# Last layer of a two-layer kernel: the down products of the experts with the weights stationary and 512 rows moving, and the row groups as the outer loop of an expert

## The chip, the cores and the metric

One NeuronCore of a Trainium2 chip runs the whole program. The metric is device time in microseconds of one execution, as the median of several runs. Names of engines: PE is TensorE, DVE is VectorE, ACT is ScalarE, POOL is GpSimd, SP is SyncE, whose queue issues most transfers.

## The reference

The program computes two layers over x of 8 x 256 rows (2048 rows, 16 tiles of 128) and 256 columns. The first layer is an attention with gates and a routed mixture of 32 experts. The second is a long convolution with two small networks, and after it a dense mixture of 8 experts, in which each row goes through every expert. The change touches that last part alone:

```python
x = hidden_states
router_probs = softmax(x @ w_router)
gate_weights = softmax(x @ w_gating / GATE_TEMP)
g = einsum('bsh,ehf->ebsf', x, w_gate)
u = einsum('bsh,ehf->ebsf', x, w_up)
h = silu(g) * u
expert_out = einsum('ebsf,efh->ebsh', h, w_down)
cw = router_probs * gate_weights
cw = cw / (sum(cw, axis=-1, keepdims=True) + 1e-09)
out = einsum('ebsh,bse->bsh', expert_out, cw)
```

The hidden width is F = 1024 per expert. The input of this part is a layer norm of x, and the result is added to x.

## The kernel before

The program is written engine by engine, with the order of every engine's instructions set by hand and semaphores between them. The last layer is reached after some 700 us.

Each expert's three matrices lie in DRAM cut into four chunks of 256 hidden units (128 x 1536 numbers: gate, up, down). A chunk is loaded by SP into one of two slots of `wS` (`load`, L423), rounded to a high half `wH` by ACT (`split_high`, L1371), and POOL takes the rest as a low half `wL` (`split_low`, L1680). Every matrix product is made of three passes (high by high, high by low, low by high) with operands of type fp32r.

The loop of the last layer counts chunks, in pairs. For each chunk come the four groups of 512 rows, and for each group the chunk's two halves of 128 hidden units. One such half for one group is a step: 32 chunks x 8 = 256 steps. A step has

- on PE an up part (`up`, L1969): twelve products, weights stationary (128 x 128), 512 rows of the transposed input `xTH`/`xTL` moving, six for the gate into a bank of PSUM and six for the up matrix into another;
- on ACT a silu of the gate (`silu`, L1376) into `sg`;
- on DVE (`expert_step`, L1226, and `expert_low`, L1236) the product `hF`, its rounded half `hH` and the rest `hL`;
- on PE a down part (`down`, L1987): for each of the four row tiles of the group three products with `hH` or `hL` stationary and 256 columns of the down matrix moving, so that the sums come out with rows on partitions.

The two halves of a chunk are summed in PSUM. DVE then takes each tile's sums, times that row's router weight (a number per partition, `cw2`), and adds them to x (`mixed`, L1242), two tiles in each step. PE's order puts the ups of step s+2 ahead of the downs of step s (`experts`, L2264), so ACT and DVE have a step and more of time.

```python
for q, (h, w, s) in enumerate(((hH, wH, sH), (hL, wH, sH), (hH, wL, sL))):
    last = pe.matmul(o, h[:, b, t * P:(t + 1) * P], piece(w, s, slot, col, D),
                     start=(opens and t % 2 == 0 and q == 0), stop=(closes and q == 2), skip_group_check=True)
```

A wait of the ups asks that the product `hF` of two steps before is done, since its PSUM bank is written again. A wait of the downs asks for that step's low half. Ahead of the first steps PE still turns the last group's normalised rows (`turn("L", 3)`, L2278) and makes the router's logits of tiles 8 to 15 in two batches (`router_logits`, L2276 and L2283). After the last step DVE adds the last four tiles, and SP stores x in four pieces as the groups get ready.

## Time and profile before

| what | value |
|---|---|
| median of three runs | 1789.19 us (1787.07 to 1790.77) |
| the profiled execution | 1789.22 us |
| its span, first to last instruction | 1787.1 us |
| mean granted clock of PE | 0.967 |
| busy: PE, DVE, ACT, POOL | 93%, 67%, 27%, 25% |
| matmuls, weight loads | 9760, 9761 |

The span is what the trace shows; 2 us lie around it. Views of the trace that are used here: the page (busy times, clock), tables by stretches of time (busy time of each engine and the granted clock), the timeline (one row per instruction or run of equal instructions: start, length, engine, line, output<-inputs, shape), and the list of transfers. A matmul's length in the timeline contains time that overlaps with the next one, so PE's pace is read from start to start. The weight loads of PE have rows of their own (PEld) beside the matmuls.

### The profile page before, as it was taken

What the parts mean: (1) busy time and instruction counts of PE and PEld (TensorE: products, weight loads), DVE (VectorE), ACT (ScalarE), POOL (GpSimd) and SP (SyncE); (2) the same over time, 40 slices, a digit from 0 to 9 for tenths busy, and PEclk for the clock granted to TensorE, in tenths of its full rate; (3) what the DMA queues carried; (4) which work ended last, traced back from release to release, by engine and by line L of the source; (5) the groups of instructions that cost most, each with busy time, mean ns of one, the idle gap of its engine ahead of it and who ended that gap; (6) DMA issues with size and microseconds to landing.
All of it is one profiled execution on the core that took longest, in us unless ns stands there. A gap on an engine that the chain in (4) does not pass through costs nothing.

```text
span 1787.1 us, 29075 instructions
## 1 busy us (share of the span) xinstructions
PE 1662.3 (93%) x9760; PEld 1424.1 (80%) x9761; DVE 1203.4 (67%) x2477; ACT 478.7 (27%) x844; POOL 449.1 (25%) x297
## 2 busy tenths in 40 slices
PE   6999987698957798999999999999999999999998
PEld 5896663388845687888888888888888888888887
DVE  6666787466656795666666766766766766766765
ACT  4455332143422464211211211211111111111111
POOL 2551257688436601100100100100100100100100
PEclk9998998799978997999999999999999999999999
DMA  6993031388643200010000000000000000000001
GB/s 199 276 340 145 24 113 50 106 248 262 204 132 106 69 1 19 19 36 18 19 34 18 20 32 18 20 33 18 21 31 18 23 30 18 26 26 18 18 0 48
DMA packets 72003, 127.51 MB, mean 71 GB/s; under 512 B 8320, under 2 KB 51776, under 8 KB 71808
## 3 DMA queue, kind: packets, MB, share of 16 engines
q1 hardware_dynamic: 38096, 84.31, 14.6%
q10 hardware_dynamic: 27696, 25.51, 4.5%
q0 software_dynamic: 6144, 16.79, 2.9%
q8 instruction: 43, 0.70, 0.2%
q14 instruction: 24, 0.20, 0.0%
HBM read 82.54 MB, written 44.04 MB: 71 GB/s over the span
## 4 chain that ended last, share of the span: by engine, by line
PE 78%; POOL 6%; issue 5%; DMA 5%; DVE 4%; ACT 1%; SPq 0%; POOLq 0%; DVEq 0%; another core or an unknown queue 0%; ACTq 0%
PE ps L1982 39%; PE ps L1998 20%; PE ps L2089 4%; DMA slots_in<-xn,idS 3%; PE ps L2108 2%; POOL slots_in L1710 2%; POOL yg L1749 2%; PE ps L1781 2%; PE ps L2069 1%; PE ps L2186 1%; DMA yg<-slots_out,idG 1%; DMA x<-in_x 1%; PE ps L1851 1%; PE ps L1850 1%; PE ps L2164 1%
## 5 line engine op out<-in xcount | busy, mean ns | idle before, releaser
L1982 PE MATMUL ps<-xTH,wH 128*128 128x512 f32 x1024 | 402.8, 393 | 1.5 <-DVE hF L1231 1.5
L1982 PE MATMUL ps<-xTH,wL 128*128 128x512 f32 x1024 | 402.2, 393 | 0.0
L1982 PE MATMUL ps<-xTL,wH 128*128 128x512 f32 x1024 | 399.1, 390 | 0.0
L1379 ACT ACTIVATE sg<-ps 128x512 f32<-128x512 f32 x264 | 157.9, 599 | 884.2 <-PE ps L1982 884.2
L1231 DVE TENSOR_TENSOR hF<-sg,ps 128x512 f32<-128x512 f32 x256 | 175.9, 687 | 303.8 <-ACT sg L1379 303.8
L1682 POOL TENSOR_TENSOR wL<-wS,wH 128x1536 fp32r<-128x1536 f32 x32 | 111.8, 3495 | 961.1 <-ACT wH L1374 961.1
L1998 PE MATMUL ps<-wL,hH 128*128 128x256 f32 x1024 | 289.8, 283 | 0.0
L1998 PE MATMUL ps<-wH,hL 128*128 128x256 f32 x1024 | 289.7, 283 | 0.0
L1998 PE MATMUL ps<-wH,hH 128*128 128x256 f32 x1024 | 288.6, 282 | 0.5 <-DVE hL L1240 0.5
L1240 DVE TENSOR_TENSOR hL<-hF,hH 128x512 fp32r<-128x512 f32 x256 | 258.4, 1009 | 0.1
L1982 PEld LDWEIGHTS ps<-xTL,wH 128*128 128x128 f32 x1024 | 192.8, 188 | 42.2
L1250 DVE SCALAR_TENSOR_TENSOR x<-ps,cw,x 128x256 f32<-128x256 f32 x512 | 222.7, 477 | 1.0 <-PE ps L1998 1.0
L1982 PEld LDWEIGHTS ps<-xTH,wH 128*128 128x128 f32 x1024 | 193.8, 189 | 35.7 <-ACT sg L1379 1.4
L1982 PEld LDWEIGHTS ps<-xTH,wL 128*128 128x128 f32 x1024 | 193.9, 189 | 30.6
L1998 PEld LDWEIGHTS ps<-wH,hH 128*128 128x128 f32 x1024 | 195.5, 191 | 10.6 <-DVE hL L1240 0.7
L1998 PEld LDWEIGHTS ps<-wH,hL 128*128 128x128 f32 x1024 | 195.5, 191 | 9.9
L1998 PEld LDWEIGHTS ps<-wL,hH 128*128 128x128 f32 x1024 | 195.5, 191 | 0.0
L1234 DVE CAST hH<-hF 128x512 fp32r<-128x512 f32 x256 | 109.4, 427 | 36.7 <-PE ps L1998 28.0
L1710 POOL DMA_INDIRECT slots_in<-xn,idS x64 | 74.6, 1166 | 60.5 <-DMA slots_in<-xn,idS 30.7
L1781 PE MATMUL ps<-maskT,idb 128*128 128x384 bf16 x348 | 73.6, 343 | 15.6 <-DVE x L973 15.6
L2089 PE MATMUL ps<-eHL,hH 128*128 x384 | 81.5, 295 | 2.4 <-POOL eHL L1697 2.4
L1749 POOL DMA_INDIRECT yg<-slots_out,idG x48 | 51.2, 1067 | 71.1 <-DMA slots_out<-yo 49.0
(396 smaller groups left out, 2440.1 us busy)
## 6 DMA issues: line engine op xcount, KB each, us to landing
wS<-in_w SPq DMA_DIRECT2D x32, 768.0 KB, 4.2
slots_in<-eS SPq DMA_DIRECT2D x16, 768.0 KB, 10.6
eS<-in_wr SPq DMA_DIRECT2D x32, 384.0 KB, 4.1
xl<-slots_in ACTq DMA_DIRECT2D x48, 256.0 KB, 3.8
slots_out<-yo ACTq DMA_DIRECT2D x48, 256.0 KB, 3.0
k_parts<-parts SPq DMA_DIRECT2D x8, 512.0 KB, 5.6
q_parts<-parts SPq DMA_DIRECT2D x8, 512.0 KB, 3.9
stackA<-k_parts SPq DMA_DIRECT2D x24, 128.0 KB, 5.6
```

Source lines behind the costliest of these rows:

```text
L1231: dve.tensor_tensor(hF[:, b, :], sg[:, b, :], ps[:, 2 + b, :], ALU.mult).then_inc(mul_done, 1)
L1234: dve.tensor_copy(hH[:, b, :], hF[:, b, :]).then_inc(h_high, 1)
L1240: dve.tensor_tensor(hL[:, b, :], hF[:, b, :], f32(hH[:, b, :]), ALU.subtract).then_inc(h_low, 1)
L1250: dve.scalar_tensor_tensor(x[:, tile, :], acc, cw2[:, tile, bass.ds(it, 1)], x[:, tile, :], ALU.mult, ALU.add).then_inc(evac_done, 1)
L1379: act.activation(sg[:, b, :], ps[:, b, :], ACT.Silu).then_inc(silu_done, 1)
L1682: pool.tensor_tensor(blocks(wL, slot, plain), blocks(wS, slot, plain), f32(blocks(wH, slot, plain)), ALU.subtract).then_inc(w_low, 1)
L1710: pool.indirect_dma_start(xs_d, bass.IndirectOffsetOnAxis(ap=idS[:, n, k:k + 1], axis=0), xn[:, n, :], None, bounds_check=TILES * P - 1, o ...
L1749: pool.indirect_dma_start(slot_rows(n)[:, k, :], None, ys_d, bass.IndirectOffsetOnAxis(ap=idG[:, n, k:k + 1], axis=0), bounds_check=TILES ...
L1781: pe.matmul(ps[:, bank, 0:384], idb[:, :], maskT[:, :], start=True, stop=True)
L1982: last = pe.matmul(ps[:, 2 * half + b, :], piece(w, s, slot, col, P), v[:, k, g * 512:(g + 1) * 512], start=q == 0, stop=q == 5)
L1998: last = pe.matmul(o, h[:, b, t * P:(t + 1) * P], piece(w, s, slot, col, D), start=(opens and t % 2 == 0 and q == 0), stop=(closes and q = ...
L2089: last = pe.matmul(ps[:, 2 + b, t * D:(t + 1) * D], h[:, b, (2 * t + k) * P:(2 * t + k + 1) * P], eFlat[:, bass.ds(off + (w + k * D), D)], ...
```

## The change

The down part is turned round: the down matrix's 128 x 128 blocks are the stationary operand, and 512 rows of `hH` or `hL` move, six products a step. The sums come out transposed, with columns on partitions, and eight halves (all 1024 hidden units of an expert) are summed in PSUM for one group before they are read. For this the loops of an expert change places: the four groups are the outer loop and the eight halves the inner one, and all four chunks of the expert stay on the chip, in `wH`/`wL` and two new buffers `wH2`/`wL2` that take the place of older tensors.

DVE multiplies the sums by the router's weights, now along the free dimension (`cwB`, the expert's 2048 weights on every partition), and adds them to transposed sums `yT` in SBUF (`weigh`, `add`), in three steps of every eight. `cwB` comes from DRAM: the weights `cwc` are turned once on PE, copied by ACT, stored, and SP loads one line of 8 KB to all partitions for each expert. In the last expert PE turns the sums back (`turn_out`, eight transposes for each group) and DVE adds them to x (`add_out`); its last group keeps the old form of the down products. The first steps change their order too: the turning of the last rows and the logits, now one batch for tiles 8 to 15, stand later.

```diff
+        def chunk_high(c):
+
+            return wH[:, 1 - c, :] if c < 2 else wH2[:, c - 2, :]
...
+            def load_weights_of(e):
+
+                rows = cw_d.rearrange("(e n) p -> e (n p)", n=NT)
+                src = rows[e:e + 1] if isinstance(e, int) else rows[bass.ds(e, 1)]
+                sp.dma_start(cwB[:, :], src.to_broadcast([P, NT * P])).then_inc(cw_moved, 16)
+
+            load_chunks(0)
+            sp.wait_ge(turned_copied, 5)
+            sp.dma_start(cw_d, cwT[:, :]).then_inc(cw_moved, 16)
+            sp.wait_ge(cw_moved, 16)
+            load_weights_of(0)
+            with sp.Fori(1, E1) as e:
+                load_chunks(e)
+                sp.wait_ge(mix_read, e * 8)
+                load_weights_of(e)
...
+            def weigh(e, g, dt):
+
+                if dt == 0:
+                    dve.wait_ge(down_done, e * 32 + (8 * U_L1 + 8 * g + 8))
+                    dve.wait_ge(cw_moved, e * 16 + 32)
+                dve.tensor_tensor(tm[:, dt, :], ps[:, 4 + 2 * (g % 2) + dt, :], cwB[:, g * 512:(g + 1) * 512], ALU.mult).then_inc(mix_read, 1)
+
+            def add(e, g, dt, first):
+
+                dve.wait_ge(mix_read, e * 8 + (2 * g + dt + 1))
+                if first:
+                    dve.tensor_copy(yT[:, g, dt, :], tm[:, dt, :]).then_inc(sum_added, 1)
+                else:
+                    dve.wait_ge(sum_added, e * 8 + (2 * g + dt - 7))
+                    dve.tensor_tensor(yT[:, g, dt, :], yT[:, g, dt, :], tm[:, dt, :], ALU.add).then_inc(sum_added, 1)
...
+            def add_out(k, half):
+
+                g = (k + 3) % 4
+                dve.wait_ge(out_turned, k + 1)
                 for t in (2 * half, 2 * half + 1):
-                    tile = pair % 4 * 4 + t
-                    acc = ps[:, 4 + 2 * (pair % 2) + t // 2, (t % 2) * D:(t % 2) * D + D]
-                    dve.scalar_tensor_tensor(x[:, tile, :], acc, cw2[:, tile, bass.ds(it, 1)], x[:, tile, :],
-                                             ALU.mult, ALU.add).then_inc(evac_done, 1)
+                    acc = ps[:, 4 + 2 * (g % 2) + t // 2, (t % 2) * D:(t % 2) * D + D]
+                    dve.tensor_tensor(x[:, 4 * g + t, :], acc, x[:, 4 * g + t, :], ALU.add).then_inc(out_ready, 1)
...
+            def replace(e, c):
+
+                act.wait_ge(down_done, e * 32 + (8 * U_L1 - 32 + 24 + 2 * c + 2))
+                chunk_split(e, c)
+
+            def expert(e, first=False, last=False):
+                for s in range(32):
+                    silu(e * 32 + (8 * U_L1 + s), s % 2, PLAIN)
+                    if not first and s in (0, 2):
+                        replace(e, 2 + s // 2)
...
+                    if not last and s in (28, 30):
+                        replace(e + 1, (s - 28) // 2)
...
+                else:
+                    for dt, w, h, q in ((0, high, hH, 0), (0, low, hH, 1), (1, high, hH, 0), (1, low, hH, 1), (0, high, hL, 2), (1, high, hL, 2)):
+                        done = pe.matmul(ps[:, pair + dt, :], w[:, col + dt * P:col + (dt + 1) * P], h[:, b, :], start=(ft == 0 and q == 0),
+                                         stop=(ft == 7 and q == 2), skip_group_check=True)
+                done.then_inc(down_done, 1)
+
+            def turn_out(k):
+
+                g = (k + 3) % 4
+                pe.wait_ge(sum_added, 8 * (E1 - 1) + 2 * k)
+                for dt in range(2):
+                    for t in range(4):
+                        done = pe.transpose(ps[:, 4 + 2 * (g % 2) + t // 2, (t % 2) * D + dt * P:(t % 2) * D + (dt + 1) * P],
+                                            yT[:, g, dt, t * P:(t + 1) * P], ident[:, :])
+                done.then_inc(out_turned, 1)
+
+            def expert(e, first=False, last=False):
+
+                for s in range(32):
+                    if s < 30:
+                        expert_up(e, s + 2)
                     elif not last:
-                        expert_up(it + 1, local - 14)
-                    expert_down(it, local)
+                        expert_up(e + 1, s - 30)
+                    if first and s == 0:
+                        pe.wait_ge(logits_read, 1)
+                    if first and s == 8:
+                        pe.wait_ge(turned_copied, 5)
+                    expert_down(e, s, last)
+                    if first and s == 1:
+                        pe.wait_ge(evac_done, 4 * M_L1)
+                        turn("L", 3, bank=6)
+                    if first and s == 2:
+                        router_logits(6, 8, 8)
+                    if first and s == 5:
+                        pe.wait_ge(cw_done, 2)
+                        pe.transpose(ps[:, 7, 0:P], cwc[:, :, :].rearrange("p e n -> p (e n)"), ident[:, :]).then_inc(turned_done, 1)
+                    if last and s % 8 == 3:
+                        turn_out(s // 8)
```

PE, a step in the middle of the last layer, before: the last ups and the first three down products, which are there four times (L1982 is `up`, L1998 is `down`).

```order
L1982 MATMUL ps<-xTH,wL 128x512
L1982 MATMUL ps<-xTL,wH 128x512
L1998 MATMUL ps<-wH,hH 128x256
L1998 MATMUL ps<-wH,hL 128x256
L1998 MATMUL ps<-wL,hH 128x256
```

The same place now, with all the down products of the step (L2369 is `expert_up`, L2392 is the new form in `expert_down`) and the first up of the next:

```order
L2369 MATMUL ps<-xTH,wL 128x512
L2369 MATMUL ps<-xTL,wH 128x512
L2392 MATMUL ps<-hH,wH 128x512 [waits h_low]
L2392 MATMUL ps<-hH,wL 128x512
L2392 MATMUL ps<-hH,wH 128x512
L2392 MATMUL ps<-hH,wL 128x512
L2392 MATMUL ps<-hL,wH 128x512 x2
L2369 MATMUL ps<-xTH,wH_198 128x512 [waits mul_done,silu_done]
```

The ups stand as they stood; twelve products of 256 columns have become six of 512, and the one wait of the downs stays that for the low half.

DVE, one step in the loop before: the product, its rounded half, the two additions to x (L1250) and the low half, with the waits.

```order
L1231 TENSOR_TENSOR hF<-sg,ps 128x512 [waits silu_done]
L1232 REGISTER_ALU
L1234 CAST hH<-hF 128x512 [waits down_done,mul_done]
L1250 ISA [waits evac_done,down_done]
L1250 SCALAR_TENSOR_TENSOR x<-ps,cw_71,x 128x256
L1250 ISA
L1250 SCALAR_TENSOR_TENSOR x<-ps,cw_71,x 128x256
L1240 TENSOR_TENSOR hL<-hF,hH 128x512 [waits h_high]
```

DVE now, steps 9 to 11 of an expert, in which the first group's sums are taken (L1289 is `weigh`, L1298 is `add`):

```order
L1276 CAST hH<-hF 128x512 [waits down_done,mul_done]
L1289 TENSOR_TENSOR tm<-ps,cwB 128x512 [waits cw_moved,down_done]
L1282 TENSOR_TENSOR hL<-hF,hH 128x512 [waits h_high]
L1273 TENSOR_TENSOR hF<-sg,ps 128x512 [waits silu_done,h_low]
L1276 CAST hH<-hF 128x512 [waits down_done,mul_done]
L1289 TENSOR_TENSOR tm<-ps,cwB 128x512
L1298 TENSOR_TENSOR yT<-yT,tm 128x512 [waits sum_added,mix_read]
L1282 TENSOR_TENSOR hL<-hF,hH 128x512 [waits h_high]
L1273 TENSOR_TENSOR hF<-sg,ps 128x512 [waits silu_done,h_low]
L1276 CAST hH<-hF 128x512 [waits down_done,mul_done]
L1298 TENSOR_TENSOR yT<-yT,tm 128x512 [waits sum_added,mix_read]
L1282 TENSOR_TENSOR hL<-hF,hH 128x512 [waits h_high]
```

The two additions of every step are gone; four instructions in three of eight steps stand in their place, and the first of them waits for the load of the router's weights, ahead of that step's low half.

ACT at the end of an expert in the loop: before, one chunk was split in every eight steps; now the exchange of the chunks begins behind the silu of steps 28 and 30 (L1615 is `chunk_split`), and two more follow in the next expert.

```order
L1690 ISA
L1614 REGISTER_ALU [waits down_done]
L1615 ACTIVATE wH<-wS 128x1536 [waits stage1_loaded]
L396 REGISTER_ALU
L1455 REGISTER_ALU [waits mul_done]
L1456 ACTIVATE sg<-ps 128x512 [waits up_done]
L396 REGISTER_ALU
L1455 REGISTER_ALU [waits mul_done]
L1456 ACTIVATE sg<-ps 128x512 [waits up_done]
L1690 REGISTER_ALU
L1614 REGISTER_ALU [waits down_done]
L1615 ACTIVATE wH<-wS 128x1536 [waits stage0_loaded]
```

Two splits, two steps apart, and each waits for a down product of the expert that ends, since it overwrites that expert's chunk.

## Rows read from the trace of the kernel before

**Rows 1.** Page, part 1: engine, busy us (share of the span), instructions.
```profile
PE 1662.3 (93%) x9760; PEld 1424.1 (80%) x9761; DVE 1203.4 (67%) x2477; ACT 478.7 (27%) x844; POOL 449.1 (25%) x297
```
**Rows 2.** Table by stretches: us, each engine's busy us, clock, DMA share, GB/s.
```profile
1000.00:1200.00 200.00, 200.00 (x1149) 176.44 (x1149) 136.26 (x240) 36.55 (x54) 20.98 (x6) 1.00 0.07 24
```
**Rows 3.** Timeline of PE, one step: start, length, engine, line, operation.
```profile
1000.77 0.40 PE L1982 MATMUL ps<-xTH,wH 128*128 128x512 f32 x1
...
1003.52 0.28 PE L1998 MATMUL ps<-wH,hH 128*128 128x256 f32 x1
1003.63 0.28 PE L1998 MATMUL ps<-wH,hL 128*128 128x256 f32 x1
...
1004.95 0.40 PE L1982 MATMUL ps<-xTH,wH 128*128 128x512 f32 x1
```
**Rows 4.** Timeline of PE, 24 ups in a row, then 16 logit products.
```profile
701.49 0.40 PE L1982 MATMUL ps<-xTH,wH 128*128 128x512 f32 x1
...
704.26 0.39 PE L1982 MATMUL ps<-xTH,wH 128*128 128x512 f32 x1
...
706.98 0.18 PE L2209 MATMUL ps<-wg1HL,xTH 128*128 128x32 f32 x1
...
708.57 0.26 PE L2210 MATMUL ps<-wg1HL,xTL 128*128 128x16 f32 x1
```
**Rows 5.** Timeline of ACT and DVE beside that step.
```profile
999.54 0.60 ACT L1379 ACTIVATE sg<-ps 128x512 f32<-128x512 f32 x1 [3.58 <-PE ps L1982]
1000.17 0.69 DVE L1231 TENSOR_TENSOR hF<-sg,ps 128x512 f32<-128x512 f32 x1 [1.50 <-ACT sg L1379]
1001.04 0.43 DVE L1234 CAST hH<-hF 128x512 fp32r<-128x512 f32 x1 [0.18 <-PE ps L1998]
1001.38 0.87 DVE L1250 SCALAR_TENSOR_TENSOR x<-ps,cw,x 128x256 f32<-128x256 f32 x2
1002.17 0.68 DVE L1240 TENSOR_TENSOR hL<-hF,hH 128x512 fp32r<-128x512 f32 x1
```
**Rows 6.** Timeline of ACT and POOL, the two halves of one chunk.
```profile
1020.93 1.48 ACT L1374 ACTIVATE wH<-wS 128x1536 fp32r<-128x1536 f32 x1
1022.49 3.50 POOL L1682 TENSOR_TENSOR wL<-wS,wH 128x1536 fp32r<-128x1536 f32 x1 [29.94 <-ACT wH L1374]
```
**Rows 7.** List of transfers: count, KB each, median us from issue to landing.
```profile
wS<-in_w SPq DMA_DIRECT2D x32, 768.0 KB, 4.2
...
x<-in_x SPq DMA_DIRECT2D x2, 1024.0 KB, 14.3
FW<-in_fw SPq DMA_DIRECT2D x1, 1024.0 KB, 6.8
```
**Rows 8.** First expert: timeline of PE, and the table's row of that stretch.
```profile
710.00:715.00 5.00, 3.94 (x12) 2.96 (x11) 3.68 (x10) 2.44 (x5) 0.00 (x0) 0.50 0.01 3
711.95 0.77 PE L1982 MATMUL ps<-xTH,wH 128*128 128x512 f32 x1 [1.06 <-DVE hF L1231]
...
716.82 0.28 PE L1998 MATMUL ps<-wH,hH 128*128 128x256 f32 x1
...
729.07 0.40 PE L1982 MATMUL ps<-xTH,wH 128*128 128x512 f32 x1
```
**Rows 9.** Timeline of PE, eight transposes and the two matmuls behind them.
```profile
694.59 1.03 PE L2146 MATMUL ps<-ident,xnL 128*128 128x128 f32 x8
695.38 0.48 PE L2164 MATMUL ps<-xTH,fH 128*128 128x512 f32 x1
695.69 0.39 PE L2164 MATMUL ps<-xTH,fL 128*128 128x512 f32 x1
```
**Rows 10.** Timeline of PE and DVE, the last downs and additions.
```profile
1779.57 0.28 PE L1998 MATMUL ps<-wL,hH 128*128 128x256 f32 x1
1780.38 0.39 PE L1998 MATMUL ps<-wH,hH 128*128 128x256 f32 x1 [0.54 <-DVE hL L1240]
...
1782.12 1.66 DVE L1250 SCALAR_TENSOR_TENSOR x<-ps,cw,x 128x256 f32<-128x256 f32 x4 [1.00 <-PE ps L1998]
```

More of the change, by code:

```diff
@@ L1272, in _ @@
-            for part in range(13, 16):
-                mixed(N_L1 // 2 - 1, part // 2, part % 2)
+            body(1)
+            with dve.Fori(2, E1 - 1) as e:
+                body(e)
+            body(E1 - 1, last=True)
+            dve.wait_ge(down_done, 8 * U_L1 + 32 * E1)
+            dve.wait_ge(out_ready, 16)
+            for t in range(4):
+                tile = 12 + t
+                acc = ps[:, 6 + t // 2, (t % 2) * D:(t % 2) * D + D]
+                dve.scalar_tensor_tensor(x[:, tile, :], acc, cwc[:, E1 - 1, tile:tile + 1], x[:, tile, :], ALU.mult, ALU.add).then_inc(out_ready, 1)
@@ L1761, in _, with chunk_rest @@
                 add_residual(g)
-            split_low(U_L1, 1)
+            def chunk_rest(e, c):
+                pool.wait_ge(w_high, e * 4 + (U_L1 + c + 1))
+                pool.tensor_tensor(chunk_low(c), wS[:, 1 - c % 2, :], f32(chunk_high(c)), ALU.subtract).then_inc(w_low, 1)
+            chunk_rest(0, 0)
             add_residual(3)
-            def experts(it, last):
-                split_low(it * 2 + (U_L1 + 1), 0)
-                if not last:
-                    split_low(it * 2 + (U_L1 + 2), 1)
-            with pool.Fori(0, N_L1 // 2 - 1) as it:
-                experts(it, False)
-            experts(N_L1 // 2 - 1, True)
+            pool.wait_ge(residual_added, 4)
+            pool.wait_ge(normed["B"], 16)
+            for c in range(1, 4):
+                chunk_rest(0, c)
+            with pool.Fori(1, E1) as e:
+                for c in range(4):
+                    chunk_rest(e, c)
         @block.tensor
@@ L2255, in _, with expert_up @@
             block("B", 3, {3: ("L", 2)}, 0)
-            def expert_up(it, local):
-                up(it * 16 + (8 * U_L1 + local), local, it * 2 + (U_L1 + local // 8), 1 - local // 8, PLAIN)
-            def expert_down(it, local):
-                down(it * 16 + (8 * U_L1 + local), local, it * 8 + (M_L1 + local // 2), 1 - local // 8, local // 2 % 2,
-                     local % 2 == 0, local % 2 == 1)
-            def experts(it, last):
-                for local in range(16):
-                    if local < 14:
-                        expert_up(it, local + 2)
-                    elif not last:
-                        expert_up(it + 1, local - 14)
-                    expert_down(it, local)
+            def expert_up(e, s):
+                n, g, ft, b = e * 32 + (8 * U_L1 + s), s // 8, s % 8, s % 2
+                if g == 0 and ft % 2 == 0:
+                    pe.wait_ge(w_low, e * 4 + (U_L1 + ft // 2 + 1))
+                pe.wait_ge(silu_done, n - 1)
+                wait(pe, mul_done, n - 1 - PLAIN)
+                high, low = chunk_high(ft // 2), chunk_low(ft // 2)
+                for half in range(2):
+                    q = 0
+                    for k in range(2):
+                        col = half * BLK + k * D + ft % 2 * P
+                        for w, v in ((high, xTH), (low, xTH), (high, xTL)):
+                            last = pe.matmul(ps[:, 2 * half + b, :], w[:, col:col + P], v[:, k, g * 512:(g + 1) * 512], start=q == 0, stop=q == 5)
+                            q += 1
+                last.then_inc(up_done, 1)
@@ new lines, in expert_down @@
+            def expert_down(e, s, last=False):
+                n, g, ft, b = e * 32 + (8 * U_L1 + s), s // 8, s % 8, s % 2
+                pair = 4 + 2 * (g % 2)
+                wait_low(pe, n + 1)
+                if ft == 0:
+                    wait(pe, mix_read, e * 8 + (2 * g - 2))
+                    if last:
+                        wait(pe, out_ready, 4 * g)
+                high, low = chunk_high(ft // 2), chunk_low(ft // 2)
+                col = 2 * BLK + ft % 2 * D
+                if last and g == 3:
+                    for t in range(4):
+                        o = ps[:, pair + t // 2, (t % 2) * D:(t % 2 + 1) * D]
+                        for q, (h, w) in enumerate(((hH, high), (hL, high), (hH, low))):
+                            done = pe.matmul(o, h[:, b, t * P:(t + 1) * P], w[:, col:col + D], start=(ft == 0 and t % 2 == 0 and q == 0),
+                                             stop=(ft == 7 and q == 2), skip_group_check=True)
+                else:
+                    for dt, w, h, q in ((0, high, hH, 0), (0, low, hH, 1), (1, high, hH, 0), (1, low, hH, 1), (0, high, hL, 2), (1, high, hL, 2)):
+                        done = pe.matmul(ps[:, pair + dt, :], w[:, col + dt * P:col + (dt + 1) * P], h[:, b, :], start=(ft == 0 and q == 0),
+                                         stop=(ft == 7 and q == 2), skip_group_check=True)
+                done.then_inc(down_done, 1)
```

152 lines of the change are left out of this document (81 added, 71 removed).

## Prediction

> **What bounds the kernel now.** I read the views from the coarse to the fine. The page's list of engines has TensorE (PE) busy for 93% of the span [rows 1]. The table by stretches then shows the stage that the change rewrites: PE is busy in every microsecond at a granted clock of 1.00, the upper of its two levels (2.4 GHz), while VectorE (DVE) works 68% of the time and ScalarE (ACT) and GpSimd (POOL) under 20% [rows 2]. What is worth anything here is therefore PE's own pace, and the timeline gives it. A step (one chunk's 128 hidden units of 512 rows) starts at 1000.77, its down part at 1003.52, the next step at 1004.95 [rows 3]: 2.75 us for twelve up products of 512 columns, 1.43 us for twelve down products of 256, 4.18 us together. 256 such steps, some 1070 us, are 60% of the span. Start to start, the ups take 229 ns on the mean and the downs 119; the matmul's own "us" column overlaps its neighbours and is not used for sums.
>
> **Two prices hide in these 229 and 119 ns.** The first down product after a run of ups takes 0.11 us, not 0.12 [rows 3]. And where 24 ups follow each other with nothing between, the first twelve, which come straight after 256-column products, take 2.77 us (701.49 to 704.26), and the second twelve 2.72 (to 706.98) [rows 4]: 231 ns, then 227. So I read 227 ns as what 512 columns cost, and half of it, 113, as what 256 cost. A run of 256-column products is paced by something else, at 120 ns, and leaves a debt that the next ups pay with a few ns each. Both the 7 ns and the debt belong to the short products.
>
> **The downs, steady part.** The change turns twelve products of 256 columns into six of 512, for all steps but the last group's eight. By 227 ns a step costs 18 x 0.2267 (2.72 / 12) = 4.080 us against 4.180, 0.100 less. The three first steps are counted below, the eight last keep the old form, so 245 steps give **-24.5 us**. Bounds: if the ups kept their 229 ns and the downs took the same, 18 x 0.229 = 4.122 and the gain is 14.2 us; if all eighteen ran at the 231 ns of the first half of [rows 4], it is 5.4 us.
>
> One rule speaks against so much. By the Trainium skill ("TensorE: Matmul & The Clock Gate", Back-to-back issue gap) a matmul at the full clock costs its columns over 2.4 GHz and a fixed 2.5 ns, so halving the number of products would save only six times 2.5 ns a step, an estimated 3.7 us in all. The trace does not agree in the fixed part: 256 columns cost 120 ns in the run and 512 cost 227, a difference of 13 ns for a pair.
>
> **DVE, off the path.** It loses two additions from PSUM a step (0.87 us) and gets, per eight steps, two weighted copies of 128x512 out of PSUM and two sums in SBUF. Nearest rows: the product that reads PSUM, 0.69, and the subtraction in SBUF, 0.68 [rows 5]. That is 2.7 us per eight steps against 7.0. Its worst step then has 0.69 + 0.43 + 0.68 + 1.4 = 3.2 us of work in 4.08. The low half is ready at 1002.85 and its down starts at 1003.52 + 4.18 = 1007.70, 4.85 us later; a later half by 0.5 us is covered. Nothing.
>
> **Weights, off the path.** Before, a chunk served 33 us; now all four are exchanged around the border of two experts. In PE's steps: chunk 0 is released after step 25, ACT splits it after the silu of step 28, POOL makes its low half, and its first up stands at the start of what would be step 30. The silu of step 28 ends about 3.5 us into step 26 (it begins 0.2 us after its ups and takes 0.60 [rows 5]); with 1.48 and 3.50 us [rows 6] the low half is there 0.5 us into step 28, 6.2 us early. Chunks 1 to 3 follow two steps apart with the same margin. The load of chunk 2 may start when the low half of chunk 0 is done and must land before ACT wants it, some 11 us later; such loads take 4.2 [rows 7]. Nothing, as long as no piece is 6 us late.
>
> **The router's weights by row.** They go through PE (one transpose, 0.1 us), DRAM, and a load that writes one 8 KB line to all 128 partitions, 1 MB, once per expert, after the last weighted copy of the expert before. DVE wants it seven steps, 28.6 us, later. No row shows a load that reads one line 128 times; the 1 MB rows took 6.8 and 14.3 us [rows 7], and I take 7, hidden either way.
>
> **The start.** Up 2 of the first expert waits for DVE's first product and starts at 711.95; the clock is at 0.50 there (1.2 GHz), and the twelve last until 716.82 [rows 8]. The change moves 16 logit products (706.98 to 708.57, 1.7 us [rows 4]) and eight transposes behind it. PE does less before 711.95 then, so I take the clock to be no higher there and keep 4.87 us for up 2. Then come three downs of 1.36, two ups of 2.72, the transposes (0.88, next part) and 32 logit products (3.5): up 5 starts at 730.7 instead of 729.07 [rows 8]. **+1.7 us**; were up 2 at the full clock, it would be 2.1 us less, so -0.4.
>
> **The end.** Sums are kept transposed, so the last expert adds four times eight transposes. One such block takes 0.79 us to the next matmul's start and makes that one's gap 0.31 instead of 0.23 [rows 9]: 0.88 x 4 = **+3.5 us**, plus 0.1 for the router's weights. Before them nothing waits: the sums they read are added two steps earlier. The last down waits 0.7 us now for a low half that stands behind two additions (1779.57 to 1780.38 where 0.12 is due) [rows 10]; these additions are gone from its step: **-0.5 us**. The four last additions (1.66 us) and the last store stay.
>
> **The sum** is made against the profiled execution, 1789.2 us, which is the median of the three times too: 1789.2 - 24.5 + 1.7 + 3.6 - 0.5 = **1769.5 us**.
>
> **Rivals.** (a) The pace of the ups is not a debt but their nature, and the downs take on their 229 ns: 1789.2 - 14.2 + 4.8 = 1779.8. For it: 229 is what ups do in every step. Against it: the second half of [rows 4], with the same operands and DVE at work.
> (b) Time goes by columns, and the short products have hardly a cost of their own. Then the step saves next to nothing, and the additions at start and end remain. With the 0.01 us that the first down of a run saves against the others taken as the whole fixed cost of a step, 2.5 us come off and 4.8 are added: 1791.5, no change that counts. For it: eleven of a step's twelve downs go at 120 ns, so a cheaper one is the exception. Against it: the 0.11 us of the first down, which is half of 227. By the Trainium skill's rule named above, with its 3.7 us, the time would be an estimated 1790.3.
> (c) Slower: the load to 128 partitions. It has 28.6 us, and the low half behind DVE's wait another 4.85, so from 33.5 us on every further microsecond is a stall of PE in each of seven experts. It decides when it outweighs the 19.7 us gained: at 36.3 us the kernel is as before, at 37 us it takes 1794. For it: one source line read 128 times is in no row, and the queue that carries it also waits for DVE. Against it: the slowest 1 MB row took 14.3.
> (d) The change does not do what it says: PE's waits stand where the shorter products would gain, since each down still waits for its low half. Against it: the 4.85 us above. I count it with (b).
>
> **How the numbers follow.** A measurement of this kernel tells 0.2%, 3.6 us, from no change. The forecast has 0.77, (a) 0.12, (b) with (d) 0.06, (c) 0.05. The forecast's own spread is -2.1 for the start's clock, a microsecond for the transposes and 2 for the pace (228 ns instead of 227 would be 4.4): 1765.5 to 1774. Up to (a) it reaches 1780, and that leaves 0.11 with (b) and (c) and a little below. Faster is the forecast and (a), 0.89; of (b) most is "same", 0.05; slower is (c) and the rest of (b), 0.06.
>
> **What would show it.** Right: in the timeline the step is 4.08 us, its eighteen gaps all at 226 to 228 ns, the down part 1.36 us, and PE busy throughout at clock 1.00; four blocks of transposes of some 0.9 us in the last 130 us; POOL's low halves done 6 us before their ups; the 1 MB loads landing in 7 to 15 us; up 5 at 729 to 731. Wrong: gaps of 231 ns or more in the steady part (the debt was not the short products'), PE waiting at a border of experts for a low half or a weighted copy, or a clock under 1.00 there.

## The result and the profile after

The changed kernel takes **1773.2 us** (median of 6 runs, 1770.1 to 1778.6), the kernel before 1789.1 (6 runs, 1787.1 to 1790.8): ratio 0.9910, with a 95% interval of 0.9895 to 0.9925. The gain is 15.9 us, where 19.7 were forecast. The profiled execution of the change took 1772.32 us, its span 1770.5.

The page of the change, part 1, beside [rows 1], and from its part 6 the load of the router's weights (count, KB each, median us to landing), beside [rows 7]:

```profile
PE 1646.7 (93%) x8306; PEld 1355.8 (77%) x8306; DVE 1043.8 (59%) x2102; ACT 478.5 (27%) x845; POOL 459.8 (26%) x297
...
cwB<-expert_weights SPq DMA_DIRECT2D x8, 1024.0 KB, 4.7
```

The table by stretches of the change, first the start, then the steady part, beside [rows 8] and [rows 2]:

```profile
710.00:715.00 5.00, 3.21 (x8) 2.57 (x9) 3.95 (x5) 2.67 (x4) 2.24 (x1) 0.50 0.00 0
...
725.00:730.00 5.00, 5.00 (x37) 4.63 (x35) 2.12 (x4) 1.88 (x2) 0.00 (x0) 0.98 0.00 0
730.00:735.00 5.00, 5.00 (x16) 4.23 (x17) 1.35 (x5) 0.31 (x1) 0.00 (x0) 0.50 0.00 0
735.00:740.00 5.00, 5.00 (x20) 4.00 (x19) 1.14 (x3) 1.88 (x2) 0.00 (x0) 0.84 0.00 0
1000.00:1200.00 200.00, 200.00 (x884) 165.62 (x883) 105.09 (x172) 34.82 (x53) 15.16 (x4) 1.00 0.06 21
```

PE is still busy throughout the steady part at clock 1.00; DVE's 136 us there have become 105. In the start there is something new: 730 to 735 at half clock. The timeline of PE, change: the start, a step in the steady part, one block of transposes, and the last downs, beside [rows 8], [rows 3], [rows 9] and [rows 10].

```profile
711.79 0.77 PE L2369 MATMUL ps<-xTH,wH 128*128 128x512 f32 x1 [4.82 <-DVE hF L1273]
...
716.64 0.39 PE L2392 MATMUL ps<-hH,wH 128*128 128x512 f32 x1
...
727.06 0.18 PE L2308 MATMUL ps<-wg1HL,xTH 128*128 128x32 f32 x1
...
729.65 0.26 PE L2308 MATMUL ps<-wg1HL,xTH 128*128 128x32 f32 x1
729.76 0.34 PE L2309 MATMUL ps<-wg1HL,xTL 128*128 128x16 f32 x1
729.96 0.38 PE L2308 MATMUL ps<-wg1HL,xTH 128*128 128x32 f32 x1
...
731.25 0.77 PE L2369 MATMUL ps<-xTH,wH 128*128 128x512 f32 x1
...
736.51 0.45 PE L2392 MATMUL ps<-hH,wH 128*128 128x512 f32 x1
...
1003.32 0.39 PE L2369 MATMUL ps<-xTH,wH 128*128 128x512 f32 x1
...
1006.04 0.39 PE L2392 MATMUL ps<-hH,wH 128*128 128x512 f32 x1
...
1007.40 0.39 PE L2369 MATMUL ps<-xTH,wH 128*128 128x512 f32 x1
...
1652.04 1.04 PE L2402 MATMUL ps<-ident,yT 128*128 128x128 f32 x8
1652.83 0.47 PE L2369 MATMUL ps<-xTH,wH 128*128 128x512 f32 x1
...
1763.61 0.28 PE L2388 MATMUL ps<-wL,hH 128*128 128x256 f32 x1
1763.77 0.39 PE L2388 MATMUL ps<-wH,hH 128*128 128x256 f32 x1
```

The step is 1003.32 to 1007.40: 2.72 us of ups and 1.36 of downs, **4.08 us**, where it was 4.18. The block of transposes takes 0.79 to the next matmul's start. In the start the logit products go at 0.11 us apart until 729.76 and at 0.21 behind it; up 5 then runs at half clock to 736.51, at 0.427 us a product behind its first.

**Where the gain went.** The last layer, from its first up to the end of the span, can be cut at the start of up 6, behind the last of the logits:

| from the trace, us | first up to up 6 | up 6 to the end | together |
|---|---|---|---|
| before | 31.76 | 1053.88 | 1085.64 |
| change | 36.61 | 1032.56 | 1069.17 |
| difference | +4.85 | -21.32 | -16.47 |

### The profile page after: what moved, and what is told of

Read it like the earlier page. It is cut to its first block, busy times and chain, and to the rows that moved or that the text cites. A ratio compares the mean times of both kernels' runs of the same rounds, so it can differ in the third digit from the quotient of the medians.

```text
span 1770.5 us, 24802 instructions
## 1 busy us (share of the span) xinstructions
PE 1646.7 (93%) x8306; PEld 1355.8 (77%) x8306; DVE 1043.8 (59%) x2102; ACT 478.5 (27%) x845; POOL 459.8 (26%) x297
## 4 chain that ended last, share of the span: by engine, by line
PE 78%; POOL 6%; issue 5%; DMA 5%; DVE 4%; ACT 1%; SPq 0%; POOLq 0%; DVEq 0%; ACTq 0%
PE ps L2369 40%; PE ps L2392 19%; PE ps L2188 4%; DMA slots_in<-xn,idS 3%; PE ps L2207 2%; POOL slots_in L1805 2%; POOL yg L1844 2%; PE ps L1880 2%; PE ps L2168 1%; PE ps L2285 1%; DMA yg<-slots_out,idG 1%; DMA x<-in_x 1%; PE ps L1950 1%; PE ps L1949 1%; PE ps L2263 1%
## 5 line engine op out<-in xcount | busy, mean ns | idle before, releaser
L2369 PE MATMUL ps<-xTH,wH 128*128 128x512 f32 x1024 | 401.1, 392 | 4.8 <-DVE hF L1273 4.8
L2369 PE MATMUL ps<-xTH,wL 128*128 128x512 f32 x1024 | 400.1, 391 | 0.0
L2369 PE MATMUL ps<-xTL,wH 128*128 128x512 f32 x1024 | 400.1, 391 | 0.0
L1861 POOL TENSOR_TENSOR wL<-wS,wH 128x1536 fp32r<-128x1536 f32 x32 | 120.4, 3764 | 867.8 <-ACT wH L1615 867.8
L2369 PEld LDWEIGHTS ps<-xTH,wH 128*128 128x128 f32 x1024 | 193.3, 189 | 45.0 <-issue 5.2
L2369 PEld LDWEIGHTS ps<-xTL,wH 128*128 128x128 f32 x1024 | 193.2, 189 | 40.5
L2369 PEld LDWEIGHTS ps<-xTH,wL 128*128 128x128 f32 x1024 | 193.4, 189 | 39.9
L2392 PE MATMUL ps<-hH,wH 128*128 128x512 f32 x496 | 193.0, 389 | 0.0
L2392 PE MATMUL ps<-hH,wL 128*128 128x512 f32 x496 | 192.9, 389 | 0.0
L1282 DVE TENSOR_TENSOR hL<-hF,hH 128x512 fp32r<-128x512 f32 x256 | 176.4, 689 | 5.6
L2392 PE MATMUL ps<-hL,wH 128*128 128x512 f32 x496 | 152.7, 389 | 0.0
L1276 DVE CAST hH<-hF 128x512 fp32r<-128x512 f32 x256 | 118.5, 463 | 20.8 <-DVE hF L1273 0.8
L2392 PEld LDWEIGHTS ps<-hH,wH 128*128 128x128 f32 x496 | 93.3, 188 | 19.4
L2392 PEld LDWEIGHTS ps<-hH,wL 128*128 128x128 f32 x496 | 93.1, 188 | 19.4
L2392 PEld LDWEIGHTS ps<-hL,wH 128*128 128x128 f32 x496 | 93.1, 188 | 19.4
L2188 PEld LDWEIGHTS ps<-eHL,hH 128*128 128x128 f32 x384 | 64.3, 194 | 2.9 <-issue 2.8
```

Source lines behind the costliest of these rows:

```text
L1276: dve.tensor_copy(hH[:, b, :], hF[:, b, :]).then_inc(h_high, 1)
L1282: dve.tensor_tensor(hL[:, b, :], hF[:, b, :], f32(hH[:, b, :]), ALU.subtract).then_inc(h_low, 1)
L1861: pool.tensor_tensor(chunk_low(c), wS[:, 1 - c % 2, :], f32(chunk_high(c)), ALU.subtract).then_inc(w_low, 1)
L2188: last = pe.matmul(ps[:, 2 + b, t * D:(t + 1) * D], h[:, b, (2 * t + k) * P:(2 * t + k + 1) * P], eFlat[:, bass.ds(off + (w + k * D), D)], ...
L2369: last = pe.matmul(ps[:, 2 * half + b, :], w[:, col:col + P], v[:, k, g * 512:(g + 1) * 512], start=q == 0, stop=q == 5)
L2392: done = pe.matmul(ps[:, pair + dt, :], w[:, col + dt * P:col + (dt + 1) * P], h[:, b, :], start=(ft == 0 and q == 0), stop=(ft == 7 and q ...
```

## The experiments

Two questions: where the 0.1 us of a step comes from, and what the start lost. All kernels start from the change. The medians carry what the stages ahead of the last layer do (the first up stood between 697.1 and 712.3 us in the profiles, though the code ahead of it is the same but for a few instructions at the border), so the last layer's own duration is compared as well. For the unchanged change it was 1069.17, 1069.25 and 1069.18 us in three profiles.

### Where the step's gain comes from

The theory: a product with a weight load of its own can't follow the one before in less than some 0.12 us, whatever its columns, so fewer and longer products gain. The rivals: the gain is in what the change took off DVE or in its order of loops; or time goes by columns alone. Each of the three kernels here was run once; what is compared is the step in the trace.

**Each down product cut in two of 256 columns**, same weights, loops and sums:

```diff
-                        done = pe.matmul(ps[:, pair + dt, :], w[:, ...], h[:, b, :], start=(ft == 0 and q == 0), ...)
+                        for part in range(2):
+                            cut = slice(part * 256, (part + 1) * 256)
+                            done = pe.matmul(ps[:, pair + dt, cut], w[:, ...], h[:, b, cut], start=(ft == 0 and q == 0 and part == 0), ...)
```

> Each of the six down products of 512 columns is made as two of 256, one after the other, each with its own load of the same weights; loops, buffers, ACT, DVE and the transposes stay as in the changed kernel. Theory (the gain comes from the length of the products: 256 columns cost 120 ns in a run, 512 cost 227, and the ups behind short products pay a debt): the step goes back from 4.080 to about 4.18 us, and the time to 1773 + 245 x 0.100 = 1797 us. Rival (the gain comes from the loops, since DVE now reads PSUM in three steps of eight instead of in every one): the step stays at 4.08 us, and the time at 1773.

Measured: 1798.07 us, last layer 1093.8. The timeline of PE in this kernel, one step:

```profile
1002.91 0.40 PE L2369 MATMUL ps<-xTH,wH 128*128 128x512 f32 x1
...
1005.66 0.40 PE L2394 MATMUL ps<-hH,wH 128*128 128x256 f32 x2
1006.13 0.40 PE L2394 MATMUL ps<-hH,wH 128*128 128x256 f32 x2
...
1007.09 0.40 PE L2369 MATMUL ps<-xTH,wH 128*128 128x512 f32 x1
```

The step is 4.18 us again, with the same 0.11 us for the first product, 0.12 for the others and ups of 2.75 us as before, though operands, columns and DVE's work are those of the change. The whole gain of the steady part is gone, and the last layer is 24.6 us longer. Time by columns alone is refuted.

**Cut in four of 128 columns** (the same loop over four parts):

```diff
+                        for part in range(4):
+                            cut = slice(part * 128, (part + 1) * 128)
...
```

> Each down product of 512 columns is made as four of 128, 24 in a step. Theory A (a short product has a fixed cost of its own, some 7 ns beside its columns): 24 x 0.064 = 1.53 us for the downs, a step of about 4.28 us, a time near 1822. Theory B (a product with a load of weights cannot follow the one before it in less than some 0.11 to 0.12 us, however short it is): 24 x 0.11 to 0.12 = 2.6 to 2.9 us, a step of 5.4 to 5.6 us, a time of 2090 to 2150.

Measured: 2139.7 us. The timeline of PE, one step:

```profile
1000.98 0.45 PE L2369 MATMUL ps<-xTH,wH 128*128 128x512 f32 x1
...
1003.81 0.56 PE L2394 MATMUL ps<-hH,wH 128*128 128x128 f32 x4
1004.21 0.61 PE L2394 MATMUL ps<-hH,wL 128*128 128x128 f32 x4
...
1006.44 0.45 PE L2369 MATMUL ps<-xTH,wH 128*128 128x512 f32 x1
...
1079.65 0.50 PE L2369 MATMUL ps<-xTH,wH 128*128 128x512 f32 x1 [2.07 <-issue]
```

Four products of 128 columns take 0.40 to 0.45 us: some 0.11 each, hardly less than 0.12 for twice the columns. So there is a floor for a short product behind a short one, and products of 256 columns stand at it. The first of a run, behind an up, isn't held by it: start to start it takes 0.058 us here, half of the 0.113 that the first of 256 columns takes. The twelve ups behind the short products now take 2.83 us (1000.98 to 1003.81), where it was 2.75 with halves and 2.72 in the change. The last row is a loss of its own: at five borders of experts PE pauses for 1.6 to 2.1 us with no wait that the profile shows, and is at half clock for a while behind it; these borders cost 19 us together. What pauses PE there was not tried.

**The old form of the down products in the loops of the change**, sums by row, no transposes (`cwB` is still loaded and not used):

```diff
-                if last and g == 3:
+                if True:
                     for t in range(4):
                         o = ps[:, pair + t // 2, (t % 2) * D:(t % 2 + 1) * D]
...
-                dve.tensor_tensor(tm[:, dt, :], ps[:, 4 + 2 * (g % 2) + dt, :], cwB[:, g * 512:(g + 1) * 512], ALU.mult).then_inc(mix_read, 1)
+                for t in (2 * dt, 2 * dt + 1):
...
+                    done = dve.scalar_tensor_tensor(x[:, tile, :], acc, cwc[:, bass.ds(e, 1), tile] if ...,
+                                                    x[:, tile, :], ALU.mult, ALU.add)
+                done.then_inc(mix_read, 1)
...
-                    if last and s % 8 == 3:
-                        turn_out(s // 8)
```

> Half of the change: the loops of the change (groups outside, an expert's four chunks on the chip, eight halves summed in PSUM), but all down products in the form of before (hidden units stationary, twelve products of 256 columns), sums added to x by rows, no transposed sums and no transposes at the end. Theory (length of the products): the step is 4.18 us, the transposes' 3.6 us are saved, and the time is 1773 + 24.5 - 3.6 = 1794 us. Rival (the loops and the fewer reads of PSUM gave the gain): the step is 4.08 us and the time about 1769.

Measured: 1792.6 us, last layer 1090.3, step 4.18. The page of this kernel, part 1, and its step in PE's timeline:

```profile
PE 1665.1 (93%) x9762; PEld 1427.9 (80%) x9762; DVE 1029.2 (57%) x2086; ACT 478.1 (27%) x845; POOL 456.5 (25%) x297
```
```profile
1000.87 0.40 PE L2371 MATMUL ps<-xTH,wH 128*128 128x512 f32 x1
...
1003.62 0.28 PE L2388 MATMUL ps<-wH,hH 128*128 128x256 f32 x1
...
1005.05 0.40 PE L2371 MATMUL ps<-xTH,wH 128*128 128x512 f32 x1
```

DVE has even less to do than in the change (1029 against 1044 us), the loops are the new ones, and nothing is gained; up 6 to the end takes 1053.3 us, as before (1053.9). The order of the loops is what makes the new form possible, and gains nothing itself.

### What the start lost

The theory: the clock falls because 32 logit products, of 16 or 32 columns, stand in one batch. The rival: it falls because PE had stood idle for 4.8 us some time before (707.0 to 711.8).

**An earlier up 2**: DVE's and ACT's small work for the router and the normalisation moves behind the first product, so PE hardly waits; the batch stays whole.

```diff
             spread("L", 3)
-            roots("L", 3)
-            router_weights(0, 8, 1)
...
+                    if first and s == 0:
+                        expert_low(e, s)
+                        roots("L", 3)
+                        continue
...
                     expert_low(e, s)
+                    if first and s == 1:
+                        router_weights(0, 8, 1)
...
             exponentials(0, 8, 1)
-            normalise("L", 3)
...
                     if first and s == 1:
+                        normalise("L", 3)
                         act.wait_ge(block_added, 16)
```

> The changed kernel with another order at the start of the last layer: ACT makes the first two silus before it normalises the last group, and DVE makes the first product before that group's roots, so that PE's third up part starts some 5 us earlier. The 32 logit products stay one batch. Theory (the batch of 32 logit products by itself lets the clock fall, as it did at 729.8 us): the fall stays, and the time is that of the changed kernel less 5 for the idle and 2 for the up part at half clock: about 1766. Rival (the clock fell there because PE had idled from 707 to 712 us): no fall, and 3.5 us more are gained: about 1762.

Measured: 1769.3 us (1767.8 to 1770.3, 4 runs), ratio to before 0.9896 (0.9879 to 0.9912); last layer 1066.8. Table by stretches, and the batch in PE's timeline:

```profile
720.00:725.00 5.00, 3.16 (x20) 2.51 (x20) 4.86 (x9) 1.88 (x2) 0.00 (x0) 1.00 0.00 0
725.00:730.00 5.00, 5.00 (x24) 4.81 (x24) 1.20 (x5) 0.00 (x0) 0.00 (x0) 0.53 0.00 0
```
```profile
723.54 0.28 PE L2312 MATMUL ps<-wg1HL,xTH 128*128 128x32 f32 x1 [1.32 <-DVE xTL L1079]
...
725.24 0.28 PE L2313 MATMUL ps<-wg1HL,xTL 128*128 128x16 f32 x1
725.37 0.38 PE L2312 MATMUL ps<-wg1HL,xTH 128*128 128x32 f32 x1
```

The wait of 4.8 us at up 2 has become 0.2, and the clock falls in the batch all the same, at 725.3. The long idle is not needed for it. But there are shorter waits ahead of the batch now (1.6, 0.5 and 1.3 us). They are most of why the last layer gains 2.4 us and not 7, and why this kernel alone doesn't clear the rival wholly: the clock falls behind the 16th product here, in the change behind the 25th.

**The logits in two batches of 16**, behind the downs of steps 2 and 3:

```diff
...
                     if first and s == 2:
-                        router_logits(6, 8, 8)
-                    if first and s == 5:
+                        pe.wait_ge(xT_low, 8 + 2 * len(TURNS))
+                        router_logits(6, 8, 4)
+                    if first and s == 3:
+                        router_logits(7, 12, 4)
+                    if first and s == 6:
```

> The changed kernel with its batch of 32 logit products cut in two of 16, behind the steps 2 and 3 of the first expert. Theory (32 such products in a row let the clock fall, 16 do not): no fall at 730 us, 0.9 us for the slowed logits and 2.6 for the up part at half clock come back: 1773 - 3.5 = 1769 to 1770. Rival (the clock falls there for what happened before, the idle from 707 to 712): unchanged, 1773.

Measured: 1773.8 us (1767.2 to 1780.1), last layer 1066.0, 3.2 less than the change. The idle of 4.8 us ahead of up 2 is still in it. Table by stretches over both batches (738.0 to 739.7 and 743.9 to 745.6):

```profile
735.00:740.00 5.00, 5.00 (x32) 4.46 (x31) 3.18 (x7) 0.60 (x1) 0.00 (x0) 1.00 0.00 0
740.00:745.00 5.00, 5.00 (x29) 4.27 (x28) 2.39 (x8) 1.88 (x2) 0.00 (x0) 1.00 0.00 0
```

With the idle kept and the batch halved the clock stays at its upper level, so the idle alone doesn't make it fall here: in this start it takes the batch of 32. That the batch alone would be enough is not shown, since no kernel has it without either the idle or the shorter waits ahead. By its median this run would speak for the rival; the stages ahead of the last layer put it there (the first up of its profile stands at 712.3 us), and the layer itself is shorter.

**The order of before in the start**, with the rest of the change:

```diff
+            pe.wait_ge(logits_read, 1)
+            router_logits(5, 8, 4)
+            pe.wait_ge(evac_done, 4 * M_L1)
+            turn("L", 3, bank=6)
             expert(0, first=True)
...
+                    if first and s == 1:
+                        router_logits(6, 12, 4)
...
-                    if first and s == 2:
-                        router_logits(6, 8, 8)
...
```

> One part undone: the first steps of the last layer in the order of the kernel before, logits in two batches of 16 products and the last group turned before the third up part; all else as changed. Theory (the start lost 2 us by its order and 2.6 us more by the clock that fell in the batch of 32 logit products): the sixth up part starts near 729 us at the full clock, and the time is 1773 - 4.5 = 1768 to 1769. Rival (the missing gain is elsewhere): 1772 to 1774.

Measured: 1769.6 us (1766.2 to 1778.2), ratio 0.9893 (0.9870 to 0.9916); last layer 1065.3, 3.9 less than the change. So of the 4.85 us that the new start costs, 3.9 come back with the old order; the rest, 1.0, stays in a wait for DVE's product ahead of up 3 that the kernel before doesn't have. The new order gains nothing. The change as it is, **run again** beside these:

> The changed kernel itself, unchanged, beside the next three on one chip. Theory (its time varies by the clock at the start of the last layer, which falls once or twice for some microseconds): times spread over 1769 to 1779 again, median near 1773, while the kernel before spreads over 4 us at most. Rival (the spread was chance): within 4 us.

It took 1776.7 us (1771.9 to 1781.3), ratio 0.9926 (0.9906 to 0.9947). The spread is there again, but the kernel before, beside it, spread over 8 us (1787.1 to 1795.2) and not 4, and the start of the last layer isn't its source: the clock falls twice there in all three profiles of the change, and the layer's duration is the same to 0.1 us.

### A better start

**Both edits together** (the earlier up 2 and the two batches, the diffs above; the second exponentials a step later):

```diff
-            roots("L", 3)
-            router_weights(0, 8, 1)
...
-                        router_logits(6, 8, 8)
+                        router_logits(6, 8, 4)
+                    if first and s == 3:
+                        router_logits(7, 12, 4)
...
-                    if first and s == 4:
-                        exponentials(8, 8, 2)
+                    if first and s == 5:
+                        exponentials(8, 8, 3)
```

> Both repairs of the start together: the first silus and the first product earlier, and the logits in two batches. Theory: no idle from 707 to 712 us, no fall of the clock there or at 730: 5 + 2 + 3.5 us come back, the time is 1762 to 1763. Rival (what is gained at the start is lost again at a wait behind it, for the routed weights or a low half): 1766 or more.

Measured: 1767.1 us (1766.4 to 1773.1), ratio 0.9876 (0.9856 to 0.9896); last layer 1065.2: 4 us gained, not the sum of the two, as the rival had it. PE at up 2, ACT, DVE and POOL in its start, and the table over the end of the first batch of logits:

```profile
711.89 0.47 PE L2375 MATMUL ps<-xTH,wH 128*128 128x512 f32 x1 [0.19 <-DVE hF L1271]
```
```profile
709.07 1.28 ACT L1462 ACT_TABLE_LOAD   x1 [2.82 <-PE ps L2375]
```
```profile
718.51 3.46 DVE L1146 TENSOR_TENSOR cwc<-sc,sm 128x64 f32<-128x64 f32 x1
...
722.73 2.83 DVE L1274 CAST hH<-hF 128x512 fp32r<-128x512 f32 x1
```
```profile
718.37 6.92 POOL L1867 TENSOR_TENSOR wL<-wS,wH 128x1536 fp32r<-128x1536 f32 x2 [17.02 <-ACT wH L1621]
```
```profile
730.00:735.00 5.00, 5.00 (x22) 4.19 (x22) 2.09 (x7) 0.00 (x0) 0.00 (x0) 0.66 0.00 0
```

The exponentials make ACT load its table again for the silu, 1.28 us ahead of DVE's first product, though PE waits only 0.19 us for that product at up 2. And a product of 64 columns takes 3.46 us on DVE while POOL splits two chunks in a row; PE waits for what is behind it (1.6, 0.5 and 1.3 us), and the clock falls at 731.4, behind a batch of 16. Hence the last try: **both exponentials behind step 5, and chunk 2 split ahead of the first step**, meant to have POOL done before DVE's small work. ACT's order in it, against the change (DVE's `router_weights(0, 8, 1)` goes behind step 6, the rest is as in both edits):

```diff
-            exponentials(0, 8, 1)
-            normalise("L", 3)
+            act.wait_ge(block_added, 16)
+            chunk_split(0, 2)
...
                     if first and s == 1:
-                        act.wait_ge(block_added, 16)
-                        chunk_split(e, 2)
+                        normalise("L", 3)
...
                     if first and s == 5:
+                        exponentials(0, 8, 1)
                         exponentials(8, 8, 3)
```

> The start once more, with the two waits away that the last trace showed: both exponentials of the router stand together behind step 5, so that no change of ACT's table lies before the first silu, and chunk 2 is split before the first step, so that POOL's split no longer covers DVE's first small operations; logits in two batches. Theory (what kept PE waiting were the table load of 1.3 us and the 3.5 us that DVE's reads of SBUF last while POOL splits): up part 2 follows the first two without a gap, the sixth up part (up 5) starts some 21 us after the first instead of 30, and the last layer is 9 to 10 us shorter than the changed kernel's 1069.2; time near 1763. Rival (the clock falls in the stretch of logits and transposes whatever their order): 3 us of it are lost again, 1766.

The change, run again beside it:

> The changed kernel itself beside it on the same chip, to compare the two with the same state of the stages before. Both theories: 1772 to 1777, with the last layer at 1069 us in the trace.

Measured: **1763.6 us** (1762.0 to 1764.0, 5 runs) against 1770.9 for the change (1768.0 to 1773.6) and 1789.2 for before: ratios to before 0.9848 (0.9827 to 0.9869) and 0.9898 (0.9878 to 0.9917). The last layer takes 1060.4 us against 1069.2, 8.7 less where 9 to 10 were expected; the change's median came out below the 1772 to 1777 expected of it. PE's timeline at up 2, those of POOL and DVE ahead of it, and the table over the second batch of logits:

```profile
708.36 0.47 PE L2374 MATMUL ps<-xTH,wH 128*128 128x512 f32 x1 [1.30 <-DVE hF L1271]
```
```profile
700.58 3.50 POOL L1866 TENSOR_TENSOR wL<-wS,wH 128x1536 fp32r<-128x1536 f32 x1 [3.62 <-ACT wH L1620]
```
```profile
700.73 3.50 DVE L1130 TENSOR_TENSOR sc<-sc,sm 128x128 f32<-128x128 f32 x1
```
```profile
725.00:730.00 5.00, 5.00 (x32) 4.42 (x30) 2.33 (x6) 2.19 (x3) 0.00 (x0) 1.00 0.00 0
```

One wait of 1.3 us is left in the start, and the clock is at its upper level throughout. The wait is longer than the 0.19 us of both edits, so there the table load cost PE 0.2 us at most. The split that was moved ahead now covers another small product of DVE, which takes 3.50 us (0.29 in both edits), and DVE works without a break from there to its first product `hF`; that this makes the wait was not tried. From the first up to up 2 the try takes 6.93 us against 5.82, and from up 2 to up 6 20.87 against 26.75: the gain is in the three waits behind up 2 and in the clock. First up to up 6, and up 6 to the end, in the profile of each kernel with the new form:

| kernel | first up to up 6 | up 6 to the end |
|---|---|---|
| change | 36.61, 36.73, 36.65 | 1032.56, 1032.52, 1032.53 |
| earlier up 2 | 34.30 | 1032.53 |
| logits in two batches | 33.36 | 1032.64 |
| order of before | 32.76 | 1032.51 |
| both edits | 32.57 | 1032.63 |
| both, exponentials and split moved | 27.80 | 1032.65 |

The second column is the same to 0.14 us: everything that these edits did lies in the start.

## Why the prediction was nearly right

- **The pace (-24.5): right.** The step came down from 4.180 to 4.080 and keeps 4.080 in every step of the new form that nothing is added to. 227 ns was the price of 512 columns, and the 229 was a debt of the short products: the cut in halves brings back both the 0.12 and ups of 2.75 us, and the cut in four makes the ups 2.83. The debt is shown; what it consists of is not.
- **Rival (b), time by columns, and the rule that speaks for it: refuted.** Twelve products of 256 instead of six of 512 cost 0.100 us a step, 17 ns for each product more. By the Trainium skill's rule ("TensorE: Matmul & The Clock Gate", Back-to-back issue gap) it would be 2.5 ns, but the section gives that for an isolated product and not for a stream of them with weight loads, as here; the measurement decides. Rival (a) falls with the gaps of 226 to 227 ns.
- **The end: right.** The three blocks in the steady part cost 0.91 us each, the last 0.87, so 3.60 against 3.5; the turn of the router's weights 0.12 against 0.1; the last down follows at 0.16 where it stood 0.81 behind, so -0.65 against -0.5. From up 6 to the end 21.3 us were gained, and 24.5 - 3.6 + 0.5 = 21.4 were forecast.
- **The start (+1.7): the step that failed.** "Then come three downs of 1.36, two ups of 2.72, the transposes (0.88, next part) and 32 logit products (3.5): up 5 starts at 730.7". It stood at 731.25, and the 32 products took 4.19 us, since the clock fell inside them; and up 5's own twelve products, which the sum left at full clock, took 5.26 instead of 2.72. Together +4.85 instead of +1.7, 3.15 us more. The profiled execution misses the forecast by 2.8 us, so the start accounts for all of that; the median misses it by 3.7, and where the other 0.9 lies no trace shows. I had asked about the clock at up 2 alone, where the table of before showed 0.50, and right there it was as forecast (711.79 to 716.64, 4.85 against 4.87).
- **DVE, nothing: right, and closer than thought.** PE waits for no low half from up 6 on, so rival (d) falls too. But of the 4.85 us of cover I had counted on, POOL takes 3.05 in six steps, which the sum left out. The timeline of DVE, and of POOL, in one of them:

```profile
987.61 0.68 DVE L1289 TENSOR_TENSOR tm<-ps,cwB 128x512 f32<-128x512 f32 x1
988.21 3.73 DVE L1298 TENSOR_TENSOR yT<-yT,tm 128x512 f32<-128x512 f32 x1
991.86 0.68 DVE L1282 TENSOR_TENSOR hL<-hF,hH 128x512 fp32r<-128x512 f32 x1
```
```profile
987.89 3.50 POOL L1861 TENSOR_TENSOR wL<-wS,wH 128x1536 fp32r<-128x1536 f32 x1 [4.26 <-ACT wH L1615]
```

  This low half is done at 992.54, and its down starts at 993.80.
- **The weights, nothing: right.** POOL's timeline at the border of two experts:

```profile
963.41 3.88 POOL L1861 TENSOR_TENSOR wL<-wS,wH 128x1536 fp32r<-128x1536 f32 x1 [102.58 <-ACT wH L1615]
```

  This low half is there at 967.29, and its first up starts at 974.7: 7.4 us early, 6.2 were forecast.
- **Rival (c), the load to 128 partitions: not so.** It lands in 4.7 us (4.3 to 5.6), less than the 7 that I took, and has 28.6.

## What to carry to other kernels

Where PE is busy throughout, look at its gaps by shape: if two short products cost more than one of twice the columns, turn the product round so that the longer side moves, even if a few transposes have to bring the sums back. When work is moved, follow the granted clock through every stretch in which the moved products stand alone, not only where it is low already; here a batch of 32 small products without a wait among them cost 0.7 us more than counted and 2.5 in the up part behind it, and the same products in two batches between long ones cost only their own time where PE had not waited just ahead of them. What is moved off a wait should also be checked for whom it then meets on the other engines: two edits that gained 2.4 and 3.2 us gave 4.0 together until the work that they ran into was moved as well, and then 8.7.

## What the runs showed that was not expected

- **The clock falls with no wait of PE.** In the change PE has no idle time from 725 to 735 us and yet falls to half clock behind 25 logit products in a row (727.06 to 729.65); it is back at 736.6. It did so in all three profiles of the change, and in the three kernels that cut or undo the down products and keep this start. In batches of 16 it held where no wait stood just ahead (logits in two batches, and the last try). With waits of 1.6, 0.5 and 1.3 us ahead it fell behind 16 products twice (earlier up 2, at 725.3; both edits, at 731.4). In the kernel before it fell at 709.5, 0.7 us behind its first batch of 16 and a wait of 0.4. So a batch of 16 is not safe by itself: what stands around it counts too, and no run here separates the two further.
- **DVE blocked by POOL.** In the kernel before, too, one low half of nearly every chunk took five times its time (timeline of DVE, before):

```profile
989.63 3.47 DVE L1240 TENSOR_TENSOR hL<-hF,hH 128x512 fp32r<-128x512 f32 x1
```

  POOL's split ran from 989.05 to 992.55. 30 of the 248 low halves from 745 us on started inside a split and took 3.47 us, the other 218 took 0.68. In the change it is one copy and six sums of `yT` (3.47 and 3.73 us, where 0.42 and 0.68 are usual). The products `hF`, which read PSUM, take 0.69 us inside and outside. The Trainium skill has it ("SBUF — State Buffer", Who interferes with whom): a DVE instruction with two inputs in SBUF contends with a GpSimd instruction that reads SBUF, and the one that comes second waits for all of the other. The trace agrees for the low halves and the sums, which have two inputs in SBUF, and shows it for the copy, which has one.
- **The floor.** Some 0.11 us for a product of 128 columns with its own weight load behind another short one, 0.120 for 256 in a run, 0.227 for 512. Whether the weight load or the issue of the pair sets it wasn't tried.
- **The spread** comes, in the profiles, from ahead of the last layer. In the profile with the logits in two batches the clock fell in an earlier stage; its table by stretches, and that of the change:

```profile
170.00:175.00 5.00, 5.00 (x11) 2.85 (x10) 4.31 (x16) 2.88 (x7) 0.00 (x0) 0.50 0.00 0
```
```profile
170.00:175.00 5.00, 5.00 (x19) 3.04 (x18) 4.56 (x25) 2.83 (x7) 0.00 (x0) 1.00 0.00 0
```

  Its first up stood at 712.26 us, that of the change at 701.34, and it took 1780.1 us in that execution with a last layer of 1066.0. A difference of a few us between medians says little there; the duration of the stage that was edited says it to 0.1.
